# Slices of x loaded, kept and split one loop iteration ahead, from the seventh iteration on, in a cross-attention and LayerNorm kernel

## What is computed

```python
qs = (q @ wq)...; ks_ = (k @ wk)...; vs = (v @ wv)...      # q is x, k and v are ctx
scores = einsum('bhqd,bhkd->bhqk', qs, ks_) / sqrt(HD)
scores = where(mask[:, None, :, :], -inf, scores)
attn = einsum('bhqk,bhkd->bhqd', softmax(scores, axis=-1), vs)
out = attn.reshape(Bq, Lq, H * HD) @ wo + q
mu, var = mean(out), mean((out - mu) ** 2)
return (out - mu) / sqrt(var + EPS) * gamma + beta
```

## Time and profile before

| | before |
|---|---|
| median of 3 runs | 677.32 us (677.12 to 677.45) |
| the profiled execution | 678.04 us, of which 676.3 us is the span of the profile |
| TensorE busy (matmuls) | 616.6 us, 91% |
| VectorE, ScalarE, GpSimd busy | 521.6, 510.6, 493.3 us (77%, 76%, 73%) |
| mean granted TensorE clock | 0.968 of full speed |

### The profile page before, as it was taken

One profiled execution on the slowest core, in us unless ns is written; L12 is line 12 of the kernel. 1 busy time (PEld: TensorE's weight loads), 2 busy tenths in 40 slices (PEclk: granted clock), 3 DMA queues, 4 the chain that ended last, 5 costly groups with the idle time before them and its releaser, 6 DMA issues.

```text
span 676.3 us, 12773 instructions
## 1 busy us (share of the span) xinstructions
PE 616.6 (91%) x3856; PEld 484.2 (72%) x3856; DVE 521.6 (77%) x1060; ACT 510.6 (76%) x1558; POOL 493.3 (73%) x640
## 2 busy tenths in 40 slices
PE   8999969899898998989899898989989898998995
PEld 6887757777676787767678676767867676777663
DVE  6677757968787786878869687886868878688887
ACT  6788748868787896877779687787868779587851
POOL 4577347867868777786977778697777869667784
PEclk9999979989998998999999899999989999998998
DMA  8522345444544343344434344443434443452102
GB/s 280 160 63 76 103 130 147 119 132 120 136 133 134 102 140 113 116 142 127 139 95 132 100 133 136 116 152 108 131 96 123 138 136 89 130 150 86 44 36 109
DMA packets 60756, 82.02 MB, mean 121 GB/s; under 512 B 22544, under 2 KB 23056, under 8 KB 60688
## 3 DMA queue, kind: packets, MB, share of 16 engines
q1 hardware_dynamic: 60688, 81.21, 40.9%
HBM read 39.53 MB, written 16.78 MB: 83 GB/s over the span
## 4 chain that ended last, share of the span: by engine, by line
PE 57%; DVE 13%; POOL 12%; issue 6%; SPq 5%; ACT 4%; DMA 2%; POOLq 0%; DVEq 0%
PE bank L424 20%; PE bank L523 18%; PE bank L462 6%; PE bank L473 5%; PE bank L496 4%; POOL pn L973 3%; POOL xl L958 3%; DVE pr L782 2%; POOL y L997 2%; DVE nm L788 2%; PE bank L501 2%; SPq L280 2%; PE bank L477 2%; ACT pr L630 2%; POOL pn L975 2%
## 5 line engine op out<-in xcount | busy, mean ns | idle before, releaser
L630 ACT ACTIVATE pr<-pr,nm 128x77 f32<-128x77 f32 x1024 | 270.5, 349 | 59.4 <-DVE nm L788 55.8
L973 POOL TENSOR_TENSOR pn<-pr,rec 128x512 f32<-128x512 f32 x128 | 135.0, 1055 | 126.4 <-DVE rec L797 90.2
L782 DVE SCALAR_TENSOR_TENSOR pr<-msk,bank 128x308 f32<-128x308 uint8 x256 | 109.5, 469 | 83.4 <-PE bank L462 78.1
L424 PE MATMUL bank<-xh,wqh 128*128 128x512 f32 x256 | 108.9, 425 | 43.5 <-POOL xl L958 43.5
L795 DVE TENSOR_REDUCE sm<-pr 128x8 f32<-128x616 f32 x128 | 100.6, 786 | 16.9 <-ACT pr L630 16.3
L424 PE MATMUL bank<-xl,wqh 128*128 128x512 f32 x256 | 106.5, 416 | 0.0
L424 PE MATMUL bank<-xh,wql 128*128 128x512 f32 x256 | 106.0, 414 | 0.0
L788 DVE TENSOR_REDUCE nm<-pr 128x8 f32<-128x616 f32 x128 | 101.8, 795 | 4.4
L462 PE MATMUL bank<-ks,qs 128*128 128x234 f32 (+1 forms) x672 | 103.2, 290 | 2.0 <-DVE pr L782 2.0
L523 PE MATMUL bank<-woh,ah 128*128 128x512 f32 x256 | 103.2, 403 | 1.5 <-DVE al L804 1.4
L601 ACT ACTIVATE ptr<-bank 128x512 f32<-128x512 f32 (+1 forms) x256 | 96.1, 430 | 10.8 <-PE bank L473 10.7
(11 more groups left out here) (85 smaller groups left out, 927.7 us busy)
## 6 DMA issues: line engine op xcount, KB each, us to landing
qs<-qs SPq DMA_DIRECT2D x336, 64.0 KB, 2.0
xraw<-xT SPq DMA_DIRECT2D x58, 256.0 KB, 3.8
xres<-x SPq DMA_DIRECT2D x58, 256.0 KB, 2.7
out<-y SPq DMA_DIRECT2D x56, 256.0 KB, 2.3
ptr<-xT SPq DMA_DIRECT2D x6, 256.0 KB, 9.7
zt<-x SPq DMA_DIRECT2D x6, 256.0 KB, 4.2
out<-zt SPq DMA_DIRECT2D x6, 256.0 KB, 2.0
ks<-khc SPq DMA_DIRECT2D x36, 38.5 KB, 2.0
```

The source lines that it names most:

```text
L424: last = nc.tensor.matmul(misc_bank(("q", i))[:], w[:, k, m * P:(m + 1) * P], s[:, blk % 2, k, :], start=(k == 0 and n == 0), stop=(k == K ...
L630: last = nc.scalar.activation(s, s, ACT.Exp, bias=nm[:, t % 2, h:h + 1], scale=1.0)
L782: nc.vector.scalar_tensor_tensor(out=pr[:, 4 * g:4 * g + 4, :], in0=msk[:, m % MR, t % 4, :].unsqueeze(1).broadcast_to([P, 4, LK]), scalar ...
L973: nc.gpsimd.tensor_tensor(pn[:, half, 0:4, :].rearrange("p s (e k) -> p (s e) k", e=2), pr[:, hs, 0:KM], rec[:, t % 2, hs].unsqueeze(2).br ...
```

## The change

A constant `XDUE = 6` is added. Iterations up to 6 do what they did. Then, at the end of iteration 6, each of the three engines does one slice more: SP issues `load_slice(16)`, ACT `keep_x(15)` and POOL `low_x(15)`. From iteration 7 on each handles the slice one further on than before: SP `load_slice(t + 10)`, ACT `keep_x(t + 9)`, POOL `low_x(t + 9)`. Places in the body, buffers and all other work stay. The number of slices stays 64, so the last iteration that handled one (54 for the load, 55 for the other two) has none now.

```diff
+XDUE = 6
@@ sync
             for t in range(T + LAG):
-                if t >= 1 and t + 9 < 4 * NBLK:
-                    load_slice(t + 9)
+                n = t + 9 + (t > XDUE)
+                if 1 <= t and n < 4 * NBLK:
+                    load_slice(n)
...
                 if t in KS_AT:
                     place_k(*KS_AT[t])
+                if t == XDUE:
+                    load_slice(t + 10)
@@ scalar
                 if t >= 2:
                     keep_pt(t - 2, 1)
-                if 1 <= t and t + 8 < 4 * NBLK:
-                    keep_x(t + 8)
+                n = t + 8 + (t > XDUE)
+                if 1 <= t and n < 4 * NBLK:
+                    keep_x(n)
...
                 exps(t, 1)
+                if t == XDUE:
+                    keep_x(t + 9)
@@ gpsimd
                     gain_and_shift(t - LAG - 2)
-                if t + 8 < 4 * NBLK:
-                    low_x(t + 8)
+                n = t + 8 + (t > XDUE)
+                if n < 4 * NBLK:
+                    low_x(n)
...
                 normalise(t, 0)
+                if t == XDUE:
+                    low_x(t + 9)
```

## The result

The changed kernel takes 629.90 us (median of 4, 628.87 to 632.09) against 677.22 us (median of 4) before: a ratio of 0.9307, 95% interval 0.9282 to 0.9332, that is 47.3 us or 7% less. The prediction was 634 us, in a range of 627 to 648. The profiled execution took 628.87 us with a span of 627.1 us; before it was 678.04 and 676.3 us.

A forecast was written before the change was run, and what follows sets the result against it. The prediction took PE, busy 91% of the span, as the bound, its main gap being waits for POOL's xl. Terms: 678.04 - 35.9 (waits) - 12.2 (slow clock) + 4 (turn) = 633.9, forecast 634 us, range 627 to 648.

The forecast's parts named there:

- The twelve waits: PE's waits of about 3 us for POOL's xl before project_q at each block's head would go: -35.9 us.
- Nothing next in line: In each block, ACT, DVE and POOL lateness would fit three slacks of 1 to 1.5 us, giving PE no new wait: 0.
- The slow stretches: Eight slow clock stretches on PE behind the block-head waits, 1.53 us each, would go with them: -12.2 us.
- Loads: SP's slice loads, issued an iteration (9 us) before use and landing in 3.9 us, would cause no steady wait: price 0.
- The turn: At iteration 6, waits for the loads of slices 15 and 16 would delay PE's transposes: +3.9 us, taken as +4.
- The sum: Whole kernel, the profiled execution plus all terms: 678.04 - 35.9 - 12.2 + 4 = 633.9 us, forecast as 634 us.

The follow-up runs named there:

- experiment 4: The kernel before the change, with only POOL's low_x(t + 8) moved ahead of gain_and_shift, no slice taken earlier: 632.82 us, ratio 0.9348.
- experiment 5: The changed kernel, with PE asking for one slice more than it needs before each block's first q projection, from q part 12 on: 678.46 us, ratio 1.0017.
- Experiment 6: The changed kernel with SP's load shift undone, so slice t + 9 is loaded only at the head of the iteration that takes it: 701.06 us, one run.
- turns 7, 8 and 10: The changed kernel with only XDUE set to 7, 8 or 10 in place of 6: 628.62, 626.81 and 633.69 us.
- experiment 7: The kernel with XDUE = 10, with slice 20's load moved ahead of the six place_k DMAs in SP's iteration 10: 625.92 us, ratio 0.9245.

## Why the prediction was right, step by step

- **The twelve waits.** Predicted -35.9 us, all twelve gone. Measured: 12 x (38.80 - 35.56) = 38.9 us, the 38.80 being the period from 176.65 to 215.45 in the trace before. This is the largest error of the sum. The idle time in the profile runs from the modelled end of the matmul before, and what PE loses runs from start to start: the earlier trace rows alone gives 3.91 us from scores to first matmul, where 0.75 us is what it takes without a wait, so 3.16 us, and the matmul behind a wait is followed 0.31 us later instead of 0.24. Together 3.23 us, not 3.0. The rows for it were in hand. In experiment 4 the same arithmetic holds: idle time 0.4 us, period 36.20 - 35.56 = 0.64 us longer.
- **Nothing next in line.** Predicted price 0, from three slacks of 1 to 1.5 us. Right: no wait in 12 blocks, and by the windows ACT works 31.40 of 35.56 us. DVE, late by 0.9 us in that step, now starts `mask_max` of the first half without a wait (it had 2.14 us of idle time there), and still waits for PE at the scores of the second half, as the step had it, 0.69 us instead of 1.71:

```profile
284.05 0.85 DVE L790 SCALAR_TENSOR_TENSOR pr<-msk,bank 128x308 f32<-128x308 uint8 x2
...
287.02 0.86 DVE L790 SCALAR_TENSOR_TENSOR pr<-msk,bank 128x308 f32<-128x308 uint8 x2 [0.69 <-PE bank L467]
```

- **The slow stretches.** Predicted -12.2 us; the blocks gave 51.2 us, of which 38.9 are the waits, so 12.3. Shown by experiments 4 and 5 to hang on the waits.
- **Loads.** Predicted price 0 in the steady part; none seen there. Experiment 6 shows that the step was not idle.
- **The turn.** Predicted: PE waits before `transpose_p(6, 0)` until 95.05 and a second time until 104.3, +3.9 us, taken as 4. Measured 95.07 and 104.04, and +4.1 us; moving the turn to 8 gave 3 us of it back. One step in between was wrong and cost nothing: `project_q(12)` began at 97.72 and not at 96.5, since the transposes and scores before it ran at the low clock too (1.08 us for the four transposes), and it still ended near 101.7, as PE was back at the full clock before the end of it. The second wait, until 104.04, would have hidden up to 2.3 us more. ACT's two waits for loads in a row are there (timeline of ACT):

```profile
93.15 0.63 ACT L606 ACTIVATE xh<-xraw 128x512 fp32r<-128x512 f32 x1 [8.40 <-DMA xraw<-xT]
...
99.92 0.63 ACT L606 ACTIVATE xh<-xraw 128x512 fp32r<-128x512 f32 x1 [5.00 <-DMA xraw<-xT]
```

- **The sum.** 633.9 against 628.87 us of the profiled execution: 5.0 us too high, of which 3.0 are the size of the waits, 1.6 the end with a slow stretch less and 0.5 the start, which neither the change nor the prediction touches. Against the median, 629.90 us, it is 4.1 us too high. So every mechanism was as forecast, and the one term with a real error of size is the waits; the slow stretch less at the end can't be counted for the change, since the traces of turns 7, 8 and 10 have it.

What stays open: why a stretch of slow clock follows some waits of 3 us and not others, and why the executions of the changed kernel spread from 628.87 to 632.09 us. Their mean clocks don't tell: the executions of 630.07 and 632.09 us both have 0.984. A slow stretch more or less at the end is worth 1.5 us between the traces of these kernels, with one trace each, so differences of that size between the variants are not explained by the place of the turn.

## What to carry to other kernels

When the busiest engine shows the same gap once per block, look at what the releasing engine did just before: if that is other work in its queue, moving the piece ahead of it shrinks the gap (here from 3.0 to 0.4 us), and making it one iteration earlier removes it; count the gap from start to start, and what the clock loses behind it too. When a piece is moved one iteration ahead, move its DMA with it: here the same change without the earlier load took 701.06 us. The iteration in which the schedule turns does the work of two, so put it where the DMA queue has room and no other burst of issues, and check what stands between the additional load and its user.

## What the runs showed of the hardware that was not expected

The granted clock behind a wait of 3.0 us followed a fixed pattern. Of the twelve waits before, the second, fifth, eighth and eleventh had no slow stretch and all others had one; of the eleven in experiment 5 again the second, fifth, eighth and eleventh had none. Each cost about 1.5 us. Behind twelve waits of 0.40 to 0.43 us (experiment 4) there was none at all. But a wait of 3 us isn't needed: in the written-out end of the kernel before, waits of 1.02 and 1.36 us had one behind them, while in the trace of experiment 7 the same two waits had none. PE's timeline, first of the kernel before, then of experiment 7:

```profile
618.65 1.38 PE L462 MATMUL bank<-ks,qs 128*128 128x156 f32 x6 [1.02 <-DVE pr L782]
...
568.17 0.99 PE L467 MATMUL bank<-ks,qs 128*128 128x156 f32 x6 [1.02 <-DVE pr L790]
```

Nor did each slow stretch cost 1.5 us. From the last `project_q` of the loop to the end of the span the changed kernel, with a slow stretch behind the wait of 1.02 us, took 71.61 us, and experiment 7, with none, 71.58: without it PE only waits 1.82 us a little later, where with it there is no such wait. The one behind the wait of 1.36 us does cost: with it the same stretch takes 73.1 to 73.2 us.
